# Second attention of a Perceiver-like model: first block of keys projected ahead of the queries, its weights split earlier, queries placed bank by bank

## The reference

```python
# end of layer 0: eight experts with 1024 hidden units
for e in range(n_experts):
    w_e = jnp.sum(top_w * (top_i == e).astype(top_w.dtype), axis=-1)
    h = jax.nn.gelu(flat_x @ W1[e] + b1[e], approximate=True)
    eo = h @ W2[e] + b2[e]
    out = out + eo * w_e[:, None]
...
# start of layer 1: x = x + _L1_xattn_ref(_layernorm(x), ctx_768, Wq, Wk, Wv, Wo, bo), 16 heads of 64
q = x @ Wq
k = context @ Wk
v = context @ Wv
sim = jnp.einsum('bhid,bhjd->bhij', q, k) * SCALE
attn = jax.nn.softmax(sim, axis=-1)
```

## Time and profile before

| | |
|---|---|
| median of 3 runs | 1471.01 us (1468.67 to 1472.4) |
| profiled execution, its own time | 1472.92 us |
| its span (first to last instruction) | 1470.9 us |
| PE busy | 1362.7 us, 93% |
| DVE busy | 1031.2 us, 70% |
| ACT busy | 1105.8 us, 75% |
| share of PE in the chain that ended last | 79% |
| mean granted clock of PE | 0.974 of full |

### The profile page before, as it was taken

The page is one execution under the profiler, slowest core; times in us unless marked ns, Lnnn a source line. Parts: engine busy times, 40 slices in busy tenths (PEclk is TensorE's granted clock), DMA queues, the critical chain, the costliest instruction groups (busy, mean ns, idle before and its releaser), DMA issues.

```text
span 1470.9 us, 37205 instructions
## 1 busy us (share of the span) xinstructions
PE 1362.7 (93%) x15348; PEld 900.3 (61%) x15348; DVE 1031.2 (70%) x1504; ACT 1105.8 (75%) x1637; POOL 109.6 (7%) x150
## 2 busy tenths in 40 slices
PE   5888887999999898999999979999999999999969
PEld 2444443677776695333333357777777777777758
DVE  6999999000001405999999988888888888888842
ACT  3777876899996335888888868888887888888810
POOL 6323211000000005000000000000000000000000
PEclk7999999999999899999999999999999999999979
DMA  4454435676765383556655567777777677899630
GB/s 141 143 190 173 157 140 157 187 177 148 178 151 169 107 278 125 188 188 222 224 186 189 189 135 135 145 144 152 152 151 151 123 139 145 174 201 185 164 124 5
DMA packets 128846, 236.51 MB, mean 161 GB/s; under 512 B 9293, under 2 KB 114215, under 8 KB 128679
## 3 DMA queue, kind: packets, MB, share of 16 engines
q1 hardware_dynamic: 128678, 234.13, 60.1%
HBM read 155.98 MB, written 78.12 MB: 159 GB/s over the span
## 4 chain that ended last, share of the span: by engine, by line
PE 79%; DVE 11%; issue 5%; ACT 3%; DMA 1%; SPq 1%; POOL 0%; POOLq 0%; DVEq 0%; ACTq 0%
PE ps L754 78%; DVE small L1479 4%; DVE W L1413 3%; DMA W<-in_ctx_dram 1%; DVE p L1413 1%; ACT W L1231 1%; DVE W L1443 1%; ACT p L1246 0%; DVE q_all L1413 0%; DVE ctxT_b L1465 0%; ACT ps L1208 0%; ACT p L1208 0%; DVE att L1413 0%; PE ps L1072 0%; DVE ctxT_a_lo L1469 0%
## 5 line engine op out<-in xcount | busy, mean ns | idle before, releaser
L1413 DVE TENSOR_TENSOR p<-ps,p 128x512 f16<-128x512 f32 (+1 forms) x467 | 350.9, 752 | 62.0 <-ACT ps L1208 59.7
L1208 ACT ACTIVATE p<-ps 128x512 f16<-128x512 f32 (+1 forms) x490 | 329.2, 682 | 79.2 <-PE ps L754 76.8
L754 PEld LDWEIGHTS ps<-q_all,W 128*128 128x128 f16 (+1 forms) x3544 | 228.7, 99 | 66.2 <-issue 11.5
L754 PE MATMUL ps<-q_all,W 128*128 128x128 f16 (+2 forms) x3544 | 262.3, 226 | 4.4 <-DVE p L1413 2.4
L1208 ACT ACTIVATE ps<-ps 128x512 f32<-128x512 f32 x392 | 235.8, 602 | 0.0
L754 PE MATMUL ps<-v,p 128*128 128x130 f16 x3136 | 168.9, 206 | 8.4 <-DVE p L1413 4.6
L754 PE MATMUL ps<-wv,ctxT_a_hi 128*128 128x512 f16 (+1 forms) x588 | 155.1, 345 | 9.7 <-DVE W L1443 5.9
L754 PEld LDWEIGHTS ps<-v,p 128*128 128x128 f16 x3136 | 146.8, 97 | 15.3 <-ACT ps L1208 6.0
L1413 DVE TENSOR_TENSOR v<-ps,v 128x512 f16<-128x512 f32 x196 | 135.5, 692 | 16.2 <-ACT v L1304 3.8
L1580 DVE COPY att<-ps 128x512 f32<-128x512 f32 x1 | 0.7, 692 | 205.2 <-PE ps L754 205.2
L754 PE MATMUL ps<-wv,ctxT_b 128*128 128x512 f16 (+1 forms) x504 | 136.6, 339 | 0.0
(11 more groups left out here) (246 smaller groups left out, 1853.5 us busy)
## 6 DMA issues: line engine op xcount, KB each, us to landing
W<-keys_hi SPq DMA_DIRECT2D x54, 896.0 KB, 8.0
W<-keys_low SPq DMA_DIRECT2D x27, 896.0 KB, 11.8
keys_hi<-p SPq DMA_DIRECT2D x75, 224.0 KB, 1.9
keys_low<-p SPq DMA_DIRECT2D x75, 224.0 KB, 1.9
keys_hi<-W SPq DMA_DIRECT2D x65, 224.0 KB, 1.9
keys_low<-W SPq DMA_DIRECT2D x65, 224.0 KB, 1.9
W<-values SPq DMA_DIRECT2D x14, 960.0 KB, 9.3
W<-in_L_ffn_W_dram SPq DMA_DIRECT2D x10, 1024.0 KB, 9.4
```

The costliest lines, as they stand in the source:

```text
L754: return pe.matmul(out_, lhsT, rhs, start=start, stop=stop, **kw)
L1208: return act.activation(out_, in_, ACT.Exp, scale=scale)
L1413: return dve.tensor_tensor(out_, a, b, op)
```

## The change

Four things are done. The key weights get an order and a semaphore of their own: SP loads Wk ahead of Wq, ACT scales it ahead of the last expert's GELU and DVE makes the rest ahead of the addition of expert 6. PE projects key block 0 directly after the last expert's down product, ahead of turning xn; ACT's and DVE's outputs of that block stand ahead of their work on the queries, and the loops of the first pass begin one turn later (`DONE`). The queries are placed bank by bank: PE signals after each half of Wq, and ACT and DVE work in four instructions of half the width each. SP's load of Wv waits for the second signal; POOL's memset waits for the layernorm's power as well, since `wk_made` now comes earlier.

```diff
@@ sync
             sp.wait_ge(exp_summed, 5)
+            load_split(ld_wk, L1.wk, d["L1_xattn_Wk"])
             load_blocks(ld_w, L1.wq, d["L1_xattn_Wq"])
-            load_split(ld_w, L1.wk, d["L1_xattn_Wk"])
-            sp.wait_ge(q_projected, 3)
+            sp.wait_ge(q_projected, 4)
             sp.wait_ge(wk_made, 2)
@@ gpsimd
             rsqrt_var(3)
+            pool.wait_ge(ln_rstd, 4)
             pool.wait_ge(wk_made, 2)
...
-            pool.wait_ge(q_hi, 4)
+            pool.wait_ge(q_hi, 6)
@@ tensor
-                    if L is L0 or i == L.nI - 1:
+                    if L is L0 or i % 4 == 3:
                         ins.then_inc(q_projected, 1)
...
+                    if i < DONE[L.n]:
+                        continue
...
+            project_keys(L1, 0, PAIR1[0])
             turn_xn(3, 6)
             project_q(L1)
             attend1()
@@ scalar
+            def scale_wk():
+                act.wait_ge(ld_wk, WK_IN[1])
+                act.wait_ge(rows_blank, 2)
+                wk_b = L1.wk[0:CB, 1024:2048]
+                act.activation(L1.wk16[:, 0, :], L1.wk[:, 0:1024], ACT.Copy, scale=VS)
+                act.activation(L1.wk16[0:CB, 2, :], wk_b, ACT.Copy, scale=VS)
+                act.activation(L1.wk16[CB:P, 2, :], wk_b, ACT.Copy, scale=VS).then_inc(wk_scaled, 1)
+
             for e in range(NE):
+                if e == NE - 1:
+                    scale_wk()
                 gelu0(e)
...
             copy_xnT(3, 6)
-            act.wait_ge(q_projected, 3)
+            keys_out(L1, 0, PAIR1[0])
             act.wait_ge(rows_blank, 3)
-            for j in range(2):
-                rows = slice(64 * j, 64 * (j + 1))
-                act.activation(by_head[rows, :, :, j, :], q4[rows], ACT.Copy, scale=0.125).then_inc(q_hi, 1)
+            for b in range(2):
+                act.wait_ge(q_projected, 3 + b)
+                for j in range(2):
+                    rows = slice(64 * j, 64 * (j + 1))
+                    act.activation(by_head[rows, b, :, j, :], ps[rows, 6 + b, :].rearrange("p (i q) -> p i q", i=4),
+                                   ACT.Copy, scale=0.125).then_inc(q_hi, 1)
@@ vector
             for e in range(NE):
+                if e == NE - 2:
+                    split_wk()
                 add_expert(e, 0)
             layernorm(3)
...
-            dve.wait_ge(q_hi, 4)
+            keys_low_out(L1, 0, PAIR1[0])
+            for b in range(2):
+                for j in range(2):
+                    rows = slice(64 * j, 64 * (j + 1))
+                    dve.wait_ge(q_hi, 3 + 2 * b + j)
+                    dve.scalar_tensor_tensor(out=low[0:CB, b, :, j, :],
+                                             in0=ps[rows, 6 + b, :].rearrange("p (i q) -> p i q", i=4), scalar=0.125,
+                                             in1=hi[rows, b, :, j, :], op0=ALU.mult, op1=ALU.subtract).then_inc(q_low, 1)
```

More of the change, by code:

```diff
@@ L119, in perceiver_kernel @@
         ld_keys = [sem(f"ld_keys{n}") for n in range(2)]
-        ld_wv, ld_wk0 = sem("ld_wv"), sem("ld_wk0")
+        ld_wv, ld_wk = sem("ld_wv"), sem("ld_wk")
         st_val, ld_val = ([sem(f"{name}{n}") for n in range(2)] for name in ("st_val", "ld_val"))
@@ L125, in perceiver_kernel @@
         EARLY = 40
-        PROJ_IN = (16, 4 * 16)
+        PROJ_IN, WK_IN = (16, 2 * 16), (2 * 16, 4 * 16)
         WV_IN = (2 * 16, 4 * 16)
@@ L311, in perceiver_kernel @@
         PAIR, BEFORE = (PAIR0, PAIR1), (BEFORE0, BEFORE1)
+        DONE = (0, 1)
         def is_direct(L, h):
@@ L513, in sync @@
             sp.dma_start(x[:, :], d["x"][0]).then_inc(ld_x, 16)
-            load_split(ld_wk0, L0.wk, d["L0_xattn_Wk"])
+            load_split(ld_wk, L0.wk, d["L0_xattn_Wk"])
             load_chunk(0)
@@ L664, in gpsimd @@
             rsqrt_var(0)
-            pool.wait_ge(ld_wk0, 32)
+            pool.wait_ge(ld_wk, WK_IN[0])
             split_weights16(L0.wk, L0.wk16, 256, L0.wk16[CB:P, 3, :]).then_inc(wk_made, 1)
@@ L847, in first_pass @@
                     if slot == 3 and BEFORE[L.n][i] is None:
-                        pe.wait_ge(q_low, 4) if L is L1 else pe.wait_ge(q_hi, 2)
+                        pe.wait_ge(q_low, 6) if L is L1 else pe.wait_ge(q_hi, 2)
                     if kind == "ab":
@@ L861, in first_pass @@
                         if n == 0:
-                            pe.wait_ge(q_hi, h // L.hp + 1 if L is L0 else 4)
+                            pe.wait_ge(q_hi, h // L.hp + 1 if L is L0 else 6)
                         if L is L1 and i == len(TURNS[1]) - 1:
@@ L1365, in scalar @@
                     act.copy(wT, ps[0:8, 0, 0:P]).then_inc(step_act, 1)
[L1366 to L1371, removed]
             copy_xnT(3, 6)
-            act.wait_ge(q_projected, 3)
+            keys_out(L1, 0, PAIR1[0])
             act.wait_ge(rows_blank, 3)
             by_head = q_max.rearrange("p (b i j q) -> p b i j q", b=2, i=4, j=2)
-            q4 = ps[:, 6:8, :].rearrange("p b (i q) -> p b i q", i=4)
-            for j in range(2):
-                rows = slice(64 * j, 64 * (j + 1))
-                act.activation(by_head[rows, :, :, j, :], q4[rows], ACT.Copy, scale=0.125).then_inc(q_hi, 1)
+            for b in range(2):
[4 more added lines that the diff above has]
+                                   ACT.Copy, scale=0.125).then_inc(q_hi, 1)
             attend1()
@@ L1483, in first_pass @@
                         ins.then_inc(max_reduced, 1)
-                    if 0 <= i - L.low_after < len(turns) and turns[i - L.low_after][0] == "keys":
+                    if DONE[L.n] <= i - L.low_after < len(turns) and turns[i - L.low_after][0] == "keys":
                         keys_low_out(L, turns[i - L.low_after][1], PAIR[L.n][i - L.low_after])
@@ L1730, in vector, with split_wk @@
             residual(1, PE_B2, 3)
+            def split_wk():
+                wk_a, wk_b = L1.wk[:, 0:1024], L1.wk[0:CB, 1024:2048]
+                dve.wait_ge(wk_scaled, 1)
+                dve.scalar_tensor_tensor(out=L1.wk16[:, 1, :], in0=wk_a, scalar=VS, in1=L1.wk16[:, 0, :],
+                                         op0=ALU.mult, op1=ALU.subtract)
+                for k in range(2):
+                    ins = dve.scalar_tensor_tensor(out=L1.wk16[k * CB:(k + 1) * CB, 3, :], in0=wk_b, scalar=VS,
+                                                   in1=L1.wk16[0:CB, 2, :], op0=ALU.mult, op1=ALU.subtract)
+                ins.then_inc(wk_made, 1)
@@ L1744, in vector @@
-            ins.then_inc(wk_made, 1)
-            dve.wait_ge(q_hi, 4)
-            hi, low = (t.rearrange("p (b i j q) -> p b i j q", b=2, i=4, j=2) for t in (q_max, q_two))
[L1747 to L1751, removed]
+            keys_low_out(L1, 0, PAIR1[0])
```

## The result

The change made the kernel slower. 11 runs of the changed kernel have a median of 1475.76 us (1471.98 to 1482.38), 11 of the kernel before 1471.01 (1465.51 to 1474.85). The ratio is 1.0045, with a 95% interval of 1.003 to 1.006: 4.4 to 8.8 us slower. (The medians themselves lie 4.75 us apart.) I had forecast 2.7 us faster. The mechanism that I expected to take back part of the gain is there and is larger than I made it, and the gain itself did not come, because of a collision that I had passed over in half a sentence.

What follows compares the result with a forecast made beforehand. PE, gapless in the first pass of the second attention, gains by starting its rhythm earlier: 2.9 + 2.6 + 0.5 - 2.5 - 0.8 = 2.7 us, from median 1471.01 to 1468.3; range 1464.8 to 1471.5.

Steps and rivals of the forecast that it cites:

- The mechanism that I expected to take back part of the gain: SP's queue: first key store lands behind Wo, so ACT waits before the fourth keys_out; 2.5 us lost.
- Key block 0 in the gap, and the clock: PE's layernorm idle: a 1.93 us block leaves about 0.8 us idle; full clock ends queries 2.9 us earlier.
- in front of nothing that the first pass waits for: Smaller moves, POOL's memset and its third copy of the queries: claimed to delay nothing in the first pass, cost 0.
- The clock as such: Query projection on PE: with gaps of 0.8 and 0.5 us the clock stays full, 3.73 us instead of 6.31.
- Queries bank by bank: Placing between queries and pair 0: half-width instructions take 2.0 us where 4.67 stood; 2.6 us gained with block 0.
- The gap at key block 2: PE at 575.33: the wait for block 0's rest goes, as it is made before the queries; 0.5 us gained.
- Weights ahead of the last GELU: ACT's scaling of Wk before the last expert's GELUs: ends before PE needs them at 555.72, no cost.
- The store behind Wo: First key store lands 9.65 us after the queries, behind Wo; ACT waits 2.7 us before keys_out(3), 2.5 us lost.
- The low clock after it: PE's new 2.4 us idle before pair 3: clock falls again, taken as 0.8 us lost, between 0 and 1.6.
- The row of the 2.46 us idle: PE idle at 498.95 followed by the low clock; the 32 records took 5.34 instead of 3.73, costing 1.6 us.
- 1.8 rather than 2.6: The sum the prediction gave if the low clock came sooner or later in the new idle before pair 3.
- Rival C: Slower: low clock twice, under the queries and in the new idle at keys_out(3); -1.0 us, 1472.0; C and D 0.06.

Runs made afterwards that it cites:

- The collision alone: Kernel before, with only POOL's memset of W waiting for the layernorm's power, so that it starts beside xn; 1475.47 us, ratio 1.003.
- memset behind xn: Changed kernel, with POOL's memset of W waiting for the layernorm's last step instead of its power; 1469.41 us, ratio to before 0.9998.
- both edits: Changed kernel, with POOL's memset waiting for xn and key block 0 stored ahead of the loads of Wv and Wo; 1465.29 us, ratio to before 0.9966.
- banks alone: Kernel before, with only the queries placed bank by bank in half-width instructions, signalled after each half; 1469.56 us, ratio 0.9988.
- memset in pieces: Changed kernel, with POOL's memset of W cut into eight memsets of 448 elements in the same place; 1468.73 us, ratio to before 0.9992.

## Why the prediction was wrong, point by point

- **Key block 0 in the gap, and the clock: wrong, and the step that failed.** The block fits into the idle, as said. The failing step is the one on what remains idle, 0.8 us, and with it the one that POOL's memset lies "in front of nothing that the first pass waits for". I asked who waits for the memset, and not what runs beside it at its new place. It was moved past no queue, but from behind xn to beside it, and it held xn for its own length. In place of a gain of 2.9 us at the queries' end, 1.7 were lost, since PE idled 3.68 us and the clock fell under the queries once more: 4.6 of the 7 us that lie between the forecast and the two first profiles. The collision alone costs 2.2 to 6.6 us in the kernel before, and without it the changed kernel equals before.
- **The clock as such: right once the idle is short.** With gaps of 0.83 to 1.06 and 0.55 or 0.56 us the queries take 3.81 us against 3.73 forecast, in all five kernels in which xn was short and key block 0 filled the gap.
- **Queries bank by bank: right.** 2.13 us from queries to pair 0 against 2.0 forecast.
- **The gap at key block 2: right.** 2.28 us from pair 0 to pair 1 against 2.91, 0.6 gained for 0.5.
- **Weights ahead of the last GELU: right, at no cost.** ACT waits 2.09 us for Wk, starts scaling at 546.91, and the last two GELU groups follow without a wait that reaches PE: the last three down products start 7.02 and 3.46 us apart, as before.
- **The store behind Wo: the place was right, the size too small.** It let ACT go on 10.1 to 10.3 us after the queries in the three profiles, not 9.65, and PE idled 2.9 to 3.1 us for 2.4. Moving the store took that idle away and left one of 0.87 to 0.97 us a block later.
- **The low clock after it: mis-sized.** I took half of 1.6. The cost is 4.27 + 3.10 - 2 x 2.44 = 2.5 us from pair 3 to pair 5. Dense work on both sides did not spare the clock. The row of the 2.46 us idle, with its 1.6 us, was the better guide, and even that is too low. (With the whole 1.6 the forecast's own terms give 1.9 in place of 2.7; "1.8 rather than 2.6" is a slip of 0.1.)

Of the forecast terms, 2.6 and 0.5 came as said; 2.9 became -1.7, -2.5 became -3.1, and -0.8 became -2.5: -4.2 in place of +2.7, and 4.4 by the two first profiles. Rival C named a slow outcome by two falls of the clock, and both happened. But it had the first fall after gaps of 0.8 and 0.5 us, not after a long hold of xn, and put the whole at 1.0 us slower; that it had the direction right is luck. What stays open is the gap between the 4.5 us of the profiles, or the 4.75 between the medians, and the middle of the interval, 6.6.

## What to carry to other kernels

When a wait is changed on an engine off the critical path, look at what its next instruction will then run beside. Here a 3.08 us GpSimd memset held a 0.41 us tensor_scalar in the chain for 2.84 us more. A wait on the chain's next signal avoided it, and so, nearly, did shorter pieces or another form of the VectorE instruction. When a start is made faster, find the transfers that have a deadline counted from it. A store that some buffer waits for belongs ahead of a large load that nobody needs yet. And count the clock with an idle of TensorE: in the stretches shown, idles of 2.1 to 4.5 us were each followed by the low clock, which cost 1.3 to 2.7 us more, and not more for a longer idle (1.3 us after one of 5.5).

## What the runs showed that I had not expected

A VectorE instruction can be held by a GpSimd instruction whose record begins after its own, by 0.02 to 0.03 us, for as long as that lasts: 3.25 us for 0.41. The memset itself was not lengthened (3.08 us with and without company). The same memset in eight pieces took 4.16 us in all and held xn 0.2 us.

An idle of 2.13 us amid dense work (memset behind xn, in front of pair 3) was also followed by the low clock (0.50 from 576 to 579 us, from 1.2 us after PE had taken up work again); idles of 0.97 us (both edits) and 1.83 us (banks alone) were not. Behind the same loads, the first key store let ACT go on between 9.3 us after the queries (memset behind xn) and 11.6 (memset in pieces).
